# A new order of calls on four engines in a pipelined state-space stage, and transposes that write PSUM in reading order

## What is computed

```
x = x + attention(layernorm(x))                 # one head of 128, 512x512 scores per batch
x = x + layernorm(x) + experts(rmsnorm(layernorm(x)))   # 16 experts, top 4, dense over all
# state-space stage, u = layernorm(x):
zxbcdt = u @ W_in.T                             # z 256, x 256, B 128, C 128, dt 4
dt  = softplus(dt + dt_bias)
xBC = silu(conv_b + sum_w shift(xBC, w) * conv_w[:, w])      # causal, 4 taps
dA  = exp(dt * -exp(A_log)); h = h * dA + outer(dt * x, B); y = h @ C   # scan over 512 tokens
g   = (y + x * D) * silu(z);  g = rmsnorm(g) * norm_w
x   = x + g @ W_out.T
x = x + layernorm(x) + experts(rmsnorm(layernorm(x)))
```

## Time and profile before

| | |
|---|---|
| runs | 869.90, 870.03, 875.33 us; median 870.03 |
| profiled execution | 871.93 us, span 870.2 us |
| mean granted TensorE clock | 0.966 of full speed |
| busy | PE 89%, DVE 79%, ACT 64%, POOL 32% |
| attention stage | about 0 to 149 us |
| first experts | to about 350 us |
| state-space stage | about 350 to 671 us |
| second experts | to the end |

### The profile page before, as it was taken

One profiled execution on the slowest core, in us unless ns is written; L12 is line 12 of the kernel. 1 busy time (PEld: TensorE's weight loads), 2 busy tenths in 40 slices (PEclk: granted clock), 3 DMA queues, 4 the chain that ended last, 5 costly groups with the idle time before them and its releaser, 6 DMA issues.

```text
span 870.2 us, 14840 instructions
## 1 busy us (share of the span) xinstructions
PE 770.9 (89%) x3896; PEld 617.5 (71%) x3896; DVE 688.4 (79%) x1612; ACT 553.1 (64%) x934; POOL 274.9 (32%) x417
## 2 busy tenths in 40 slices
PE   6879998789999999787888879798886899999998
PEld 3657677667888887565767768576765678888886
DVE  3478888879999998576858778787756978999996
ACT  4555665778888887536355463645524878888885
POOL 2135443601111020043445463554544600111110
PEclk9999999889999999999999999999997999999999
DMA  8000000645555552000000000000003446565552
GB/s 232 2 1 3 5 2 20 214 145 189 181 192 180 191 180 96 1 0 1 1 2 1 3 3 1 3 0 2 0 2 104 159 168 207 190 199 193 193 195 77
DMA packets 29202, 76.95 MB, mean 88 GB/s; under 512 B 4867, under 2 KB 9438, under 8 KB 29150
## 3 DMA queue, kind: packets, MB, share of 16 engines
q1 hardware_dynamic: 28996, 76.36, 26.3%
q10 hardware_dynamic: 154, 0.00, 0.0%
HBM read 73.73 MB, written 2.62 MB: 88 GB/s over the span
## 4 chain that ended last, share of the span: by engine, by line
PE 52%; DVE 17%; issue 15%; POOL 7%; ACT 6%; DMA 1%; DVEq 0%; SPq 0%; POOLq 0%; ACTq 0%
PE ps L1493 6%; PE ps L1494 6%; PE ps L1474 6%; PE ps L1495 6%; PE ps L1475 6%; PE ps L1476 6%; POOL rt_small L399 4%; DVE conv_acc L1144 3%; PE ps L1646 3%; DVE gram L1199 2%; PE ps L1329 1%; DVE xn L1089 1%; DVE s_lo L1070 1%; DVE t L942 1%; PE ps L1523 1%
## 5 line engine op out<-in xcount | busy, mean ns | idle before, releaser
L715 ACT ACTIVATE s_ring<-ps,b1T 128x512 f32<-128x512 f32 x256 | 172.9, 689 | 72.1 <-PE ps L1495 71.2
L1104 DVE SCALAR_TENSOR_TENSOR s_ring<-s_ring,top_col,r_all 128x1024 f32<-128x1024 f32 x128 | 178.0, 1390 | 38.5 <-ACT s_ring L715 33.9
L1070 DVE TENSOR_TENSOR s_lo<-s_ring,s_hi 128x1024 fp32r<-128x1024 f32 x128 | 161.6, 1262 | 0.0
L703 ACT ACTIVATE s_hi<-s_ring 128x1024 fp32r<-128x1024 f32 x128 | 134.5, 1051 | 2.7 <-DVE s_ring L1104 2.7
L1493 PE MATMUL ps<-ffn_hi,w_hi 128*128 (+1 forms) x256 | 105.2, 411 | 1.0 <-issue 1.0
L1474 PE MATMUL ps<-s_hi,w_hi 128*128 128x512 f32 x256 | 102.3, 400 | 1.4 <-DVE s_lo L1070 1.4
L1494 PE MATMUL ps<-ffn_lo,w_hi 128*128 (+1 forms) x256 | 102.8, 401 | 0.0
L1495 PE MATMUL ps<-ffn_hi,w_lo 128*128 (+1 forms) x256 | 102.7, 401 | 0.0
L1475 PE MATMUL ps<-s_lo,w_hi 128*128 128x512 f32 x256 | 102.0, 398 | 0.0
L1476 PE MATMUL ps<-s_hi,w_lo 128*128 128x512 f32 x256 | 101.6, 397 | 0.0
L451 POOL CAST rows_r<-rows_f 80x512 fp32r<-80x512 f32 x16 | 17.8, 1109 | 259.3 <-DMA rows_f<-route_dram 259.3
(11 more groups left out here) (238 smaller groups left out, 1664.3 us busy)
## 6 DMA issues: line engine op xcount, KB each, us to landing
r_all<-route_dram SPq DMA_DIRECT2D x128, 512.0 KB, 4.3
out_dram<-X SPq DMA_DIRECT2D x8, 256.0 KB, 4.1
X<-in_L_attn_a_x_dram SPq DMA_DIRECT2D x1, 1792.0 KB, 10.0
rows_f<-route_dram SPq DMA_DIRECT2D x48, 32.0 KB, 2.6
w_rows<-in_L_ffn_mlp_w_dram SPq DMA_DIRECT2D x1, 1024.0 KB, 13.2
route_dram<-route_cols SPq DMA_DIRECT2D x64, 8.0 KB, 1.4
in_rows<-in_L_attn_b_W_in_dram SPq DMA_DIRECT2D x1, 384.0 KB
X<-in_L_attn_a_x_dram SPq DMA_DIRECT2D x1, 256.0 KB, 2.8
```

Source lines behind the costliest of these rows:

```text
L703: eng.activation(s_hi[:, q % NR, :, :], s_ring[:, q % NR, :, :], ACT.Copy).then_inc(F["hi"], 1)
L715: eng.activation(s_ring[:, q % NR, e % 2, :], bank(e % 4), ACT.Silu, bias=b1T[:, e:e + 1], scale=ALPHA).then_inc(F["act"], 1)
L1070: eng.tensor_tensor(s_lo[:, q % NR, :, :], s_ring[:, q % NR, :, :], s_hi[:, q % NR, :, :].bitcast(F32), ALU.subtract).then_inc(F["lo"], 1)
L1104: eng.scalar_tensor_tensor(out=s_ring[:, q % NR, :, :], in0=s_ring[:, q % NR, :, :], scalar=top_col[:, 0:1], in1=r_all[:, q % NR, :, :], o ...
```

## The change

It has two parts. First, the bodies of `step` of the state-space stage are written in another order on PE, ACT, DVE and POOL; every call of before is there once. PE gets three waits for `u_lo` ahead of `conv`, `z_proj` and `dt_proj`, and one for `xb` in `back`. Second, three groups of transposes write PSUM with a stride so that it holds the tokens in the order in which they are read: the attention's `xn_turn` and the state-space stage's `u_turn` write every fourth column, `g_turn` writes runs that `gT_out` copies to a `gT` of four contiguous parts, one for each r. The copies out of PSUM and the weights of `out_proj` become contiguous.

```diff
-            gT = own("gT", [P, 2, SEQ])
+            gT = own("gT", [P, 2, NT, SEQ // NT])
...
-                eng.activation(xnT[:, par, :].rearrange("d (p r) -> d r p", r=NT),
-                               bank(4).rearrange("d (r p) -> d r p", r=NT), ACT.Copy).then_inc(S1["xnT"], 1)
+                eng.activation(xnT[:, par, :], bank(4), ACT.Copy).then_inc(S1["xnT"], 1)
...
-                eng.activation(uT[:, 0, PAD:].rearrange("d (p r) -> d r p", r=NT),
-                               bank(7).rearrange("d (r p) -> d r p", r=NT), ACT.Copy).then_inc(M["uT"], 1)
+                eng.activation(uT[:, 0, PAD:], bank(7), ACT.Copy).then_inc(M["uT"], 1)
...
+                w = P // NT
+                eng.activation(gT[:, :, :, c * w:(c + 1) * w],
+                               bank(5)[:, 0:2 * P].rearrange("e (j r p) -> e j r p", j=2, r=NT), ACT.Copy).then_inc(M["gT"], 1)
...
+                eng.tensor_tensor(uT[:, 1, PAD:], bank(7), uT[:, 0, PAD:].bitcast(F32),
                                   ALU.subtract).then_inc(M["u_lo"], 1)
...
-                    mm = eng.transpose(bank(4)[:, r * P:(r + 1) * P], xn[:, r, :], ident[:, :])
+                    mm = eng.transpose(bank(4)[:, r:SEQ:NT], xn[:, r, :], ident[:, :])
...
-                    mm = eng.transpose(bank(7)[:, r * P:(r + 1) * P], xn[:, r, :], ident[:, :])
+                    mm = eng.transpose(bank(7)[:, r:SEQ:NT], xn[:, r, :], ident[:, :])
...
-                    mm = eng.transpose(bank(5)[:, j * P:(j + 1) * P], gn[:, c % 2, j * P:(j + 1) * P], ident[:, :])
+                    mm = eng.transpose(bank(5)[:, j * P:(j + 1) * P].rearrange("e (r p) -> e p r", r=NT),
+                                       gn[:, c % 2, j * P:(j + 1) * P], ident[:, :])
...
-                        mm = eng.matmul(bank(at)[:, r * D:(r + 1) * D], gT[:, j, r:SEQ:NT], outT[:, j, :], start=(j == 0),
+                        mm = eng.matmul(bank(at)[:, r * D:(r + 1) * D], gT[:, j, r, :], outT[:, j, :], start=(j == 0),
```

More of the change, by code:

```diff
@@ L527, in step @@
                     ramps(i, odd, 2)
+                    ramps(i, odd, 3)
+                if third:
+                    router_chain(R2, i - 1)
+                if second:
+                    weigh(i, odd, 1)
                     gate(i, odd, 0)
-                    weigh(i, odd, 1)
                     rms(i, 0)
-                    ramps(i, odd, 3)
+                    gate(i, odd, 1)
+                    weigh(i, odd, 2)
+                    rms(i, 1)
                 if fourth:
@@ L845, in step @@
                 if second:
+                    xb_out(i, 1)
+                if first:
+                    conv_first(i + 1, 0)
+                if second:
                     xb_out(i, 2)
                     seg_exp(i, 2)
+                    square(i, 0)
+                if fourth:
+                    router_exp(R2, i - 2)
+                if first:
+                    conv_first(i + 1, 1)
+                if second:
+                    seg_exp(i, 3)
+                    square(i, 1)
                 if first:
@@ L1242, in step @@
                     ssm_stats(i + 1)
+                if third:
+                    norms(i - 1, 3)
+                if fourth:
+                    router_norm(R2, i - 2)
+                if first:
+                    ssm_xn(i + 1)
                 if second:
                     grams(i, odd, 0)
-                if third:
-                    norms(i - 1, 3)
-                if first:
-                    ssm_xn(i + 1)
-                if fourth:
-                    router_norm(R2, i - 2)
-                if second:
-                    grams(i, odd, 1)
                 if third:
@@ L1256, in step @@
                     u_low(i + 1)
+                if third:
+                    router_stats(R2, i - 1, M["x"])
                 if second:
+                    grams(i, odd, 1)
                     states(i, 0)
[L1259 to L1269 removed]
                 if fourth:
@@ L1272, in step @@
                 if second:
-                    grams(i, odd, 2)
+                    ys(i, odd, 0)
+                if fourth:
+                    router_top(R2, i - 2)
+                if first:
+                    conv_taps_of(i + 1, 0)
+                    dt_arg(i + 1)
+                if second:
+                    grams(i, odd, 2)
+                    ys(i, odd, 1)
+                    states(i, 1)
+                    norms(i, 0)
+                if first:
+                    conv_taps_of(i + 1, 1)
+                if second:
+                    grams(i, odd, 3)
+                    ys(i, odd, 2)
+                    states(i, 2)
+                    norms(i, 1)
                 if first:
@@ L1276, in step @@
                 if second:
-                    ys(i, odd, 2)
-                    norms(i, 1)
-                    states(i, 2)
-                if third:
-                    router_stats(R2, i - 1, M["x"])
-                if second:
-                    grams(i, odd, 3)
-                if fourth:
-                    router_top(R2, i - 2)
-                if second:
+                    ys(i, odd, 3)
                     norms(i, 2)
```

133 lines of the change are left out of this document (53 added, 80 removed).

## The result

The changed kernel takes **821.5 us**, median of 4 runs (817.3 to 825.4), beside 870.4 for the kernel before in the same comparison: ratio 0.9425, 95% interval 0.9367 to 0.9484. The profiled execution took 817.3, with a span of 815.6, 54.6 less than before. It is the fastest of the four, at a mean granted clock of 0.981; the other three, at 0.964 to 0.971, took 820.6 to 825.4.

The account below looks back on a forecast made before the run. DVE's own work was taken to bound the new order. Off the profiled 871.93 us went 13.8 + 18.4 + 4.6 + 2.5 + 2.7 = 42.0, giving 829.9, so 828 as the median; 8-in-10 range 812 to 848.

Parts of the forecast that it names:

- DVE as the floor of the new order: State-space loop step: DVE's own work bounds it, all five listed waits (6.6 us) find cover; chance 0.58.
- the walk: One loop step followed call by call in the new order, naming which DVE work covers each wait; leaves 30.7 us.
- Loop step 33.2: State-space loop step: 30.7 of DVE work + 1.5 + 1.0 = 33.2 us, from 37.8.
- First come-back, +1.5: Loop step: DVE instructions with two SBUF operands stand still while POOL works, 3.6 against 2.1 before; bounds 0 and 3.
- Second come-back, the tail, +1.0: End of a step: the chain from ys(i,2) to norms(i,3), some 8.5 us, makes DVE wait 1.0; bounds 0 and 3.
- The other steps, the same 4.6 each: State-space steps 0 to 2 and 7 gain as much as a loop step: 3 x 4.6 = 13.8, and 4.6.
- Ahead of step 0: Before state-space step 0: front(0) waits less, u_out and u_low get 0.4 shorter each; 2.5 us, bounds 0 and 4.
- Attention: Attention stage: contiguous xnT copy saves 0.4 in each of 8 batches; 2.7 us taken, bounds 0 and 3.2.
- `out_proj` hidden in the new order: State-space stage: PE gains 1.9 per batch, but grams(i,0) on DVE cover it, so worth nothing by itself.
- rival (b): Whole kernel: the order does nothing, only the layout pays, 24.3 us with attention, giving 846; chance 0.08.
- Strided PSUM writes at 0: Transposes, twelve per state-space step and four per attention batch: no cost taken, bounds 0 and 1.1 us per step.
- Rival (d): State-space step: early router_chain on POOL (4.1 us) delays xw and back(i,1); step 38.5, whole 874, slower; chance 0.05.

Follow-up runs that it names:

- pool_wait: The changed kernel with GpSimd's first weighting of a step made to wait for VectorE's four grams of chunk 0; 816.5 us, ratio 0.9339.
- layout_only: The kernel before, in its old order of calls, with the transposes and copies of the change; 859.6 us, ratio 0.9872.
- before_dve: The kernel before with eight more bn_stats of a constant on DVE ahead of the softplus in each step; 886.6 us, ratio 1.0167.

## Why the prediction was right

- *DVE as the floor of the new order*: right, by the waits (6.6 to 0.2 in step 3). Every cover named in the walk held in that step. Steps 5 and 6 show one short wait each; the 0.9 of step 5 is the cover of `segs`, which was too short at a lower clock.
- *Loop step 33.2*, measured 32.97, but as a sum of other terms, so its nearness is in part luck. *First come-back, +1.5*: DVE's own work in step 3 is 31.3, so 0.6 above the 30.7, inside its bounds. The mechanism was right, and the two holds that the runs could remove were near their terms: the `gram` products 1.14 for 1.1, the stash 0.70 for 1.0. What before already had was guessed at 2.1; its rows show holds, `xn` at 516 ns a piece in place of 344 and two `dt_tmp` at 0.53 in place of 0.17, but the sum over all was not measured. *Second come-back, the tail, +1.0*: 0.7 in step 6, not in steps 2 to 5. The wait for POOL's root that it named is there, in steps 0, 1, 6 and 7. *Not in the sum*: the pause where the loop goes back, whose 3.0 us the old chain hid almost wholly and by which one step is now 4.0 longer, 1.0 per step in the mean. Two terms too large and one missing made the number.
- *The other steps, the same 4.6 each*: the step that was off. Steps 0 to 2 gave 18.9 for 13.8 (4.2, 8.5 and 6.2), step 7 8.3 for 4.6. Step 2 has all the calls but not the pause, and it gave what step 3 gave, 6.2. Step 1 has fewer calls on DVE (26.4 us of work), and so has step 7 (23.9), so less holds them to the floor that sets the loop steps, while the old chain was as long in step 1 as in the loop steps (37.63), and longer in step 7. These 8.8 us are most of the 12.6 by which the profiled execution lies below the 829.9 of the sum. Between the medians it is 6.5: the profiled execution of before lay 1.9 above its median, the one of now 4.2 below.
- *Ahead of step 0*: 3.7 for 2.5. *Attention*: 2.5 for 2.7. With the loop's 19.4 the terms make 52.8 of the 54.6; the first expert stage, unchanged, came out 2.1 shorter, and the second 0.3 longer.
- *`out_proj` hidden in the new order*: true with the new layout. With 3.80 in the same place the cover fails by 1.4 and the layout is worth 1.4 to 2.0 per step, not 0.4. In the old order it was worth less than "all in the chain", 1.5 per step at the same clock for 2.7: rival (b)'s 24.3 was 11.
- *Strided PSUM writes at 0*: right. u_turn's transposes take 0.60 for four in either form. The Trainium skill, "PSUM — Partial Sum Buffer", section "Specifications (TRN2)", says that non-contiguous patterns slow matmuls significantly. For fp32 transposes of 128x128 that write every fourth column the measurement says otherwise.
- *Rival (d)*, that the early `router_chain` delays `xw`: not seen in loop steps. The opposite is what the runs show: in POOL's old order the early place is worth 18 us.
- *The lock*: the Trainium skill, "SBUF — State Buffer", section "Who interferes with whom", states two things more that the forecast didn't use: an instruction of DVE with at most one SBUF input, outside the modes that take both ports, does not contend, and `tensor_scalar`, `copy` and `cast` can enter such a mode. The runs agree with both: `X`, `uT` and `conv_acc` (one input in PSUM) were not held, `gn` (a `tensor_scalar` from SBUF) was, 0.71 beside a gate in place of 0.46. By that rule the come-back could be placed, and not only be counted.

## What to carry to other kernels

Where one engine sets the pace, look at what its instructions take beside another engine's, and place the other's long operations beside those that are not held: here one added wait and one moved call gave a further 1.5%. Costing an edit needs the waits of each step and not only a test load: the load was paid in full on the full engine and to two thirds on the old chain, and the total didn't tell these apart, since the granted clock had changed as well. Taking work off a full engine gives nothing where it had filled a latency. When steps differ in their calls, cost them apart; before a longer wait is put down to an edit, look at the granted clock just ahead of it; and look for what the old chain was hiding, like the pause where the loop goes back.

## What the runs showed of the hardware

- GpSimd holds even a tiny instruction of VectorE for what is left of its own: `to_end` (128x4) takes 0.15 alone and 0.85 (1.10 in `pool_wait`) beside a 1.3 us operation.
- An fp32 128x128 transpose costs the same with strided and contiguous PSUM writes. A weight load from every fourth column of SBUF does not: `out_proj` 3.92 or 1.95 for 16.
- Not every long instruction of GpSimd holds VectorE: four `gram` products took 1.14, as alone, beside a `rt_small` power of 1.04 us, which is only 128x4. The ones that held were 128x256 and 128x512.

```profile
459.86 1.14 DVE L1194 SCALAR_TENSOR_TENSOR gram<-segs,dt_a,cb 128x128 f32<-128x128 f32 x4
...
460.04 1.04 POOL L399 TENSOR_TENSOR rt_small<-rt_small,mhalf 128x4 f32<-128x4 f32 x1
```

- The granted clock stands at one of two levels, 1.00 or 0.50, and in the mean of a step of the changed kernel it was 0.94 to 1.00 with the same work. A stretch at 0.50 just ahead of `y_off` made that wait 3.3 us in place of 1.5 to 1.8, in each of the five places where it occurred in `layout_only` and `before_dve`.
- Where the hardware loop goes back, VectorE starts nothing for 3 us; it cost 3.1 to 4.0 us of a step in the new order, at a granted clock of 1.00, and 0.5 in the old. What the pause consists of was not tried.
